# Last feed-forward layer of a decoder on one core: gate and up products as three fp32r products of rounded halves, summed in PSUM

## The reference

```python
wg = w_gate.astype(f32) * (1 / 127)      # 768 x 256
wu = w_up.astype(f32) * (1 / 127)        # 768 x 256
wd = w_down.astype(f32) * (1 / 127)      # 256 x 768
gate = einsum('bsd,hd->bsh', x, wg)
up = einsum('bsd,hd->bsh', x, wu)
h = silu(gate) * up
x = layernorm(x + einsum('bsh,dh->bsd', h, wd))
```

## Time and profile before

| | us |
|---|---|
| median of 3 runs | 2913.15 |
| lowest, highest | 2906.86, 2916.09 |
| span of the profiled execution | 2913.3 |
| last layer, from the first conversion at 2637.5 to the end | 275.8 |

### The profile page before, as it was taken

The page is one execution under the profiler, slowest core; times in us unless marked ns, Lnnn a source line. Parts: engine busy times, 40 slices in busy tenths (PEclk is TensorE's granted clock), DMA queues, the critical chain, the costliest instruction groups (busy, mean ns, idle before and its releaser), DMA issues. The chain is left out here.

```text
span 2913.3 us, 31557 instructions
## 1 busy us (share of the span) xinstructions
PE 2502.7 (86%) x11456; PEld 1482.0 (51%) x11456; DVE 1650.9 (57%) x3416; ACT 1352.2 (46%) x1966; POOL 327.7 (11%) x299
## 2 busy tenths in 40 slices
PE   6898898857888888879999699996688888887998
PEld 3665666533333333356456456655355555554565
DVE  6656666525566566715443698987656566632222
ACT  3333334313555555532122665663477777871211
POOL 1001101000000000000156300000211111100000
PEclk8989989967999899978799899998899999998999
DMA  2000000015333333240034511211200110002000
GB/s 75 15 15 14 16 8 18 12 52 121 53 66 68 61 65 59 44 160 3 18 60 64 98 66 37 73 44 45 99 8 30 37 37 22 22 8 65 22 15 22
DMA packets 104945, 132.41 MB, mean 45 GB/s; under 512 B 21748, under 2 KB 87556, under 8 KB 104792
## 3 DMA queue, kind: packets, MB, share of 16 engines
q1 hardware_dynamic: 90440, 115.58, 14.8%
q0 software_dynamic: 11904, 14.69, 3.1%
q10 hardware_dynamic: 2448, 0.14, 0.1%
HBM read 73.69 MB, written 31.20 MB: 36 GB/s over the span
## 5 line engine op out<-in xcount | busy, mean ns | idle before, releaser
L987 DVE TENSOR_REDUCE xattn_tops<-region 128x2 f32<-128x1024 f32 x256 | 306.2, 1219 | 127.1 <-PE region L771 127.0
L924 ACT ACTIVATE xattn_probs<-region 128x1024 f32<-128x1024 f32 x256 | 256.3, 1022 | 126.3 <-PE region L760 125.1
L2143 PE MATMUL region<-psi_fT 128*128 128x512 f32 x512 | 230.9, 597 | 10.3 <-ACT psi_fT L2267 7.1
L156 PE MATMUL region<-gla_xT,weights_even 128*128 128x512 f32 (+1 forms) x416 | 199.6, 634 | 20.2 <-ACT gla_xT L248 20.2
L760 PE MATMUL region<-xattn_qs,xattn_ks 49*128 49x512 f32 x512 | 125.9, 494 | 61.9 <-DVE xattn_tops L987 31.1
L2143 PEld LDWEIGHTS region<-psi_fT 128*128 128x128 f32 x512 | 93.6, 190 | 126.4 <-issue 115.0
L156 PE MATMUL region<-mamba_xT,weights_odd 128*128 128x512 f32 x320 | 154.2, 628 | 3.6 <-DVE mamba_xh L1966 3.6
L789 PE MATMUL region<-xattn_probs,xattn_va 128*32 128x512 f32 x1024 | 143.5, 628 | 1.2 <-ACT xattn_o_T L951 1.2
L156 PEld LDWEIGHTS region<-gla_xT,weights_even 128*128 128x128 f32 (+1 forms) x416 | 77.1, 192 | 132.2 <-issue 106.1
L771 PE MATMUL region<-xattn_ks,xattn_qs 48*128 48x512 f32 x512 | 125.8, 490 | 13.2 <-DMA xattn_ks<-xattn_khi 8.9
L165 PE MATMUL region<-weights_even,gla_work 128*128 128x256 f32 x512 | 119.3, 393 | 17.6 <-DVE gla_work L631 11.0
(11 more groups left out here) (500 smaller groups left out, 5134.8 us busy)
## 6 DMA issues: line engine op xcount, KB each, us to landing
weights_even<-mamba_cs SPq DMA_DIRECT2D x32, 512.0 KB, 4.7
xattn_qs<-xattn_qhi SPq DMA_DIRECT2D x128, 64.0 KB, 2.3
xattn_ks<-xattn_khi SPq DMA_DIRECT2D x128, 64.0 KB, 2.3
moe_sums<-moe_picked SPq DMA_DIRECT2D x9, 512.0 KB, 8.7
gla_x<-in_x SPq DMA_DIRECT2D x8, 512.0 KB, 3.8
x_after_gla<-gla_res SPq DMA_DIRECT2D x8, 512.0 KB, 2.9
xattn_x<-x_after_gla SPq DMA_DIRECT2D x8, 512.0 KB, 4.1
xattn_ctxT<-in_ctxT SPq DMA_DIRECT2D x8, 512.0 KB, 4.4
```

The source lines that it names most:

```text
L156: last = st.nc.tensor.matmul(o[0:m, i, :], w[:, c, col + i * P:col + i * P + m], rhs[:, c, :], start=c == 0, stop=c == kc - 1)
L924: A_(probs[:, p % 3, a, :, :], st.region(f"k{v}")[:], ACT.Exp).then_inc(st.emptying(f"k{v}"), 1)
L987: V.tensor_reduce(tops[:, n % 2, t, a::2], st.region(f"q{u}")[:], AX, ALU.max).then_inc(st.emptying(f"q{u}"), 1)
L2143: last = mm(o[:, a, :], fT[:, h, 0, t * P:t * P + P], fT[:, h, 1 + a, :], start=True, stop=True)
```

## The change

The gate and up products take each operand as a sum of two parts of the type float32r: the high part is the rounded value, the low part what is left. A product of fp32 operands (weights w, tokens v) is replaced by three products w_hi v_hi + w_lo v_hi + w_hi v_lo, added up in the same PSUM region; w_lo v_lo is left out. DVE makes both parts of w_gate and w_up straight from the int32 weights, one pass each. ACT writes the high part of the transposed tile (`xhi`), and DVE, in a new step `low(b)`, subtracts it from the PSUM region and writes `xlo`; the region is released by DVE and no more by ACT. The conversion of w_down goes from DVE to ACT, in the place where ACT converted w_up. Silu, the down product and the norm stay as they are.

```diff
-        x, xT, h = st.sb("x", [B, NT, D]), st.sb("xT", [2, DC, T]), st.sb("h", [2, HF, T])
+        x, h = st.sb("x", [B, NT, D]), st.sb("h", [2, HF, T])
+        xhi, xlo = (st.sb(n, [2, DC, T], F32R) for n in ("xhi", "xlo"))
...
-                                pe.wait_ge(st.sem(f"wide_{n}"), 1)
+                                pe.wait_ge(st.sem(f"split_{n}"), 2)
                             for c in range(DC):
-                                last = mm(o[:, a, :], wide[n][:, c, e * P:e * P + P], xT[:, b % 2, c, :],
-                                          start=c == 0, stop=c == DC - 1)
+                                for k, (w, v) in enumerate(((whi, xhi), (wlo, xhi), (whi, xlo))):
+                                    last = mm(o[:, a, :], w[n][:, c, e * P:e * P + P], v[:, b % 2, c, :],
+                                              start=c == 0 and k == 0, stop=c == DC - 1 and k == 2)
...
-                A_(wide["w_up"][:], weights["w_up"].bitcast(I32), ACT.Copy).then_inc(st.sem("act_step"), 1)
+                A_(w_down[:], weights["w_down"].bitcast(I32), ACT.Copy).then_inc(st.sem("act_step"), 1)
                 act.wait_ge(st.sem("act_step"), nth())
-                A_(wide["w_up"][:], wide["w_up"][:], ACT.Copy, scale=1.0 / 127.0).then_inc(st.sem("wide_w_up"), 1)
+                A_(w_down[:], w_down[:], ACT.Copy, scale=1.0 / 127.0).then_inc(st.sem("w_down"), 1)
...
-                        A_(xT[:, b % 2, :, :], st.region(f"xT{b}")[:], ACT.Copy).then_inc(st.emptying(f"xT{b}"), 1)
+                        A_(xhi[:, b % 2, :, :], st.region(f"xT{b}")[:], ACT.Copy).then_inc(st.sem("xhi"), 1)
...
+                def low(b):
+                    dve.wait_ge(st.sem("xhi"), b + 1)
+                    V.tensor_tensor(xlo[:, b % 2, :, :], st.region(f"xT{b}")[:], xhi[:, b % 2, :, :].bitcast(F32),
+                                    ALU.subtract).then_inc(st.emptying(f"xT{b}"), 1)
+
                 weights.arrive(dve)
-                for n in ("w_gate", "w_down"):
-                    V.tensor_copy(wide[n][:], weights[n].bitcast(I32)).then_inc(st.sem("dve_step"), 1)
-                    dve.wait_ge(st.sem("dve_step"), nth())
-                    V.tensor_scalar(wide[n][:], wide[n][:], 1.0 / 127.0, None, ALU.mult).then_inc(
-                        st.sem(f"wide_{n}"), 1)
+                for n in ("w_gate", "w_up"):
+                    V.tensor_scalar(whi[n][:], weights[n].bitcast(I32), 1.0 / 127.0, None, ALU.mult).then_inc(
+                        st.sem(f"split_{n}"), 1)
+                    dve.wait_ge(st.sem(f"split_{n}"), 1)
+                    V.scalar_tensor_tensor(wlo[n][:], weights[n].bitcast(I32), 1.0 / 127.0, whi[n][:].bitcast(F32),
+                                           ALU.mult, ALU.subtract).then_inc(st.sem(f"split_{n}"), 1)
+                    if n == "w_gate":
+                        low(0)
                 for what, b, e in work:
-                    if what == "hidden":
+                    if what == "xT" and b:
+                        low(b)
+                    elif what == "hidden":
```

More of the change, by code:

```diff
@@ L2484, in ffn_layer @@
         ident = K["ident"]
-        x, xT, h = st.sb("x", [B, NT, D]), st.sb("xT", [2, DC, T]), st.sb("h", [2, HF, T])
+        x, h = st.sb("x", [B, NT, D]), st.sb("h", [2, HF, T])
+        xhi, xlo = (st.sb(n, [2, DC, T], F32R) for n in ("xhi", "xlo"))
         silu, shift = st.sb("silu", [2, T]), st.sb("shift", [2, NT])
         norms = [Norm(st, s) for s in range(2)]
-        wide = {n: st.sb(n, list(weights[n].shape[1:])) for n in ("w_gate", "w_up", "w_down")}
+        whi, wlo = ({n: st.sb(f"{n}_{part}", [DC, HID], F32R) for n in ("w_gate", "w_up")} for part in ("hi", "lo"))
+        w_down = st.sb("w_down", list(weights["w_down"].shape[1:]))
         def order():
@@ L2530, in _ @@
                         if b == 0:
-                            pe.wait_ge(st.sem("wide_w_down"), 1)
+                            pe.wait_ge(st.sem("w_down"), 1)
                         for e in range(HF - 3, HF):
@@ L2536, in _ @@
                             for c in range(HF):
-                                last = mm(o[:, t * D:t * D + D], h[:, b % 2, c, t * P:t * P + P], wide["w_down"][:, c, :],
+                                last = mm(o[:, t * D:t * D + D], h[:, b % 2, c, t * P:t * P + P], w_down[:, c, :],
                                           start=c == 0, stop=c == HF - 1)
```

## The result

The changed kernel takes 2887.62 us (median of 4, 2881.93 to 2890.82), against 2914.62 us for the kernel before in the same comparison (median of 4, 2906.86 to 2925.87). The ratio is 0.9893 with a 95% interval of 0.9865 to 0.9922: 27 us or 1.1% faster. That is inside the whole range of the prediction (2868 to 2890 us), but 12.6 us above its 2875 us and outside the range of its main forecast (2868 to 2883 us): it lies where rival (a) was put, which had a chance of 0.08.

A forecast was written before the change was run, and what follows sets the result against it. TensorE, without a break in the last stage, was taken as the bound. Terms -40.5 + 1.2 + 0.2 + 0.85 = -38.2 us from the 2913.15 us median gave 2875 us; main range 2868 to 2883, whole range 2868 to 2890 us.

The forecast's parts named there:

- rival (a): Gate and up matmuls: pitch is 0.24 us, as in the back-to-back fp32r rows with two loads; 2889 us; chance 0.08.
- (d): Each batch: DVE's subtraction comes onto the path, 8.5 us more, 2884 us; chance 0.04.
- TensorE sets the time of the stage: Last stage: TensorE runs without a break, so gate and up matmul time counts in full; DVE and ACT have room.
- Term 1: Gate and up products: 576 fp32r records at 0.2158 us, 124.3 us instead of 164.8 us, so 40.5 us less.
- Term 2: Start of the stage: the first matmul waits for DVE's subtraction after ACT's copy, 1.2 us more.
- Term 3: Start of the stage: 0.2 us more waiting for w_up, nothing for the slow clock; bounds 1.0 and 1.7 us.
- Each batch: The subtraction before xT's region is released is covered by 2.7 us of TensorE work, so it costs nothing.
- Term 4: End of the last batch: silu 5 still waits for ACT's apply, so 0.85 us of the gain is not had.
- (b): Gate and up matmuls: fp32r load not hidden behind the matmul before, pitch 0.406 us, 2985 us; chance 0.04.
- (c): Gate and up matmuls: fp32r on all 128 rows streams at the fp32 record's 0.429 us, 2998 us; chance 0.02.

The follow-up runs named there:

- the integer kernel: Changed kernel with weights as unscaled integers, two products instead of three, and two moves at the edges; last layer 202.9 us against 248.2 us, 2847.84 us in all.
- the kernel without that wait: Changed kernel with both weights split before the first subtraction and batch 6's apply behind hidden tile 5 of batch 7; last layer 247.5 us against 248.2 us.
- the waking matmuls: Kernel with integer weights plus three extra 512-column products on TensorE at the start of the stage; last layer 200.8 us against 202.9 us.
- the two kernels with copies: Changed kernel with two or four idle copies of the subtraction on DVE ahead of it in batches 1 to 7; last layer 248.3 and 261.2 us against 248.2 us.
- the kernel with half the load: Changed kernel with 64 instead of 128 stationary columns in gate and up products, half the hidden units left out; last layer 258.2 us against 248.2 us.

## Why the prediction was right, and where it was off

What bounds the layer was right; the size of the largest term wasn't. The measured time lies in the range because the range had been widened to take in rival (a) and (d), and not by the main forecast.

**TensorE sets the time of the stage.** Right: 27.6 us of the last layer and nothing elsewhere, and the integer kernel scaled as the count of matmuls.

**Term 1, 40.5 us less.** The mechanism was right (one record each, the load not in series with the stream), the size wrong. The step that failed is "I take 0.2158 us", the pitch of down matmuls. Measured is 0.2335 us, 576 x 0.2335 = 134.5 us, and the term is 30.3 us. The choice took the second load to be the reason for the 0.24 us; by the experiments it explains 0.0065 us of it, not 0.024 us. The fp32 records, from which 0.2158 us was taken, have 10.36 us for 48 x 256 columns in two passes, 0.42 ns a column and pass; an fp32r record streams its one pass at 0.443 ns a column, which those rows can't show. The other bound, 0.24 us, was 3% off, the chosen one 8%: the only measured row of the same type was the better guide than a finer argument over another type. Rival (a), given 0.08, was closest: 2889 us. Its gain of 24.3 us is still 3.3 us under the 27.6 us of the layer; the totals lie closer, because the median of the kernel before was 1.5 us higher in the comparison than when the forecast was made, and by scatter.

**Term 2, 1.2 us.** 1.19 us.

**Term 3, 0.2 us and nothing for the clock.** Mis-sized: the first 48 records take 13.95 us and a warm stretch 11.20 us, 2.75 us lost, where before 15.52 against 13.73 us lost 1.79 us. It is 0.96 us for both together, inside the bounds that were given. TensorE waited 0.45 us for the up halves, but the clock was the cost, as the kernel without that wait shows. The failing step is "The slow clock costs what it cost before": the first matmul starts 1.2 us later, but the clock rises 3.5 us later, 13.6 us into the layer instead of 10.1. That TensorE's longer pause (2.37 us behind the transposes instead of 1.11 us) is the reason is argued: the waking matmuls show that filling the pauses helps, not that this difference alone made it.

**Each batch.** Right. Cover of 2.7 us was forecast, 3.1 us read, and the two kernels with copies bracket it between 2.4 and 4.9 us.

**Term 4, 0.85 us.** 0.60 us, for the tile's pitch is 2.80 us and not 2.59 us.

**The sum** with the measured terms is -30.3 + 1.2 + 0.96 + 0.6 = -27.5 us, against 27.6 us measured in the layer. One more slip: the span was compared with the median as though they were the same measure. The profiled execution after has a span of 2887.8 us and a time of 2889.57 us, 1.8 us more. It changed nothing, as the forecast is the median less a difference.

**The rivals.** (b) is refuted by the pitch of 0.120 us with a load in each step: even at the rate of bfloat16 the stream of 256 columns is 0.2158 / 2 = 0.108 us of it, so 0.012 us at most is left for a load in series. The Trainium skill's page "TensorE: Matmul & The Clock Gate", Part 3, has the rule that a load overlaps a matmul in flight only on other array rows; for full-width fp32r the trace disagrees, with this 0.120 us. (c) is refuted by 0.2335 us. (d) stayed away by 3.1 us of cover.

## What to carry to other kernels

Price an operation by the row of its own type and shape, even if it is a bad one, and take a row of another type only for the bound; 0.02 us a matmul were 10 us here. Where TensorE runs without a break, splitting fp32 into fp32r parts pays by the count: 3 x 0.2335 us against 0.858 us, and 2 x 0.2335 us where one operand is exact, as integers are. Before it pays further, look at what the faster engine will wait for: here it was mostly DVE's products and subtractions, with a 2.07 us apply in ACT's queue, that took the gain of the down product, and the waits brought the slow clock back on top. So when a reordering is judged by its total, read the granted clock of each stretch first.

## What the runs showed of the hardware

- fp32r, full array, granted clock 1.00: 0.2335 us for 512 columns, 0.120 us for 256, 0.2300 to 0.231 us for 512 with a load of 64 columns; bfloat16 0.2158 us for 512. Why an fp32r stream is slower than a cycle of 2.4 GHz by 0.026 ns a column was not tried; that reading 4 bytes a column is the limit is only a guess.
- In the kernel with half the load, where the down product (fp32) has 64 rows, its last one took 19.60 us in the chain instead of 10.61 us, at a granted clock of 0.53, though TensorE was busy for all of the stretch. The kernel after has 1.00 in the like stretch, behind a pause of the same length (5.0 us from the last up record to the first down record in both). Windows of the kernel with half the load:

```profile
2840.00:2856.00 16.00, 14.50 (x64) 8.86 (x62) 5.44 (x15) 4.33 (x8) 1.26 (x2) 1.00 0.00 0
2857.00:2876.00 19.00, 19.00 (x48) 14.46 (x46) 0.00 (x0) 0.00 (x0) 0.00 (x0) 0.53 0.04 14
```

  So 9.0 of the 10.0 us that this layer is longer are the clock of its last 48 matmuls; at full clock 48 of them take 10.55 us, 0.2 us more than with 128 rows, which over seven batches is most of the rest. In the kernels with the down product in fp32r on 128 rows the clock had also fallen ahead of the last down product, and was back at 1.00 before its end (7.70 us in all against 5.97 us). Why it stayed at 0.50 with 64 rows is not shown; it is one run.
- The clock of TensorE can be raised ahead of need by matmuls whose results are thrown away: 3.3 us at the start of one layer, of which 1.2 us went again with the later landing of x.
- A wait costs more than its length where it brings the slow clock back: 48 fp32r matmuls of 256 columns took 5.70 to 6.03 us at full clock and 7.41 to 7.74 us where it had fallen, in three kernels.
